# Other query tiles for two units of weight sums, and one catch-up block of the layer norm moved behind the next pair's copies

## The reference

```python
xn = _layernorm(x)
qkv = einsum('bnd,ed->bne', xn, w_qkv)          # q, k, v of width 512
sim = q @ k^T * 512**-0.5, causal; attn = softmax(sim)
s = (attn @ v) @ w_out^T + b_out
h = silu(xn @ wg^T) * (xn @ wu^T)               # hidden 3072, w = int / 127
out = x + s * silu(h @ wd^T)
```

## Time and profile before

| what | value |
|---|---|
| three runs before: median (lowest, highest) | 1453.6 us (1452.38, 1461.93) |
| the profiled execution's own time | 1456.9 us |
| its span (slowest core, first to last instruction) | 1455.3 us |
| outside the span | 1.6 us |
| VectorE, ScalarE, GpSimd busy | 48%, 23%, 14% |
| DMA, mean | 188 GB/s, 273.82 MB |

### The profile page before, as it was taken

How to read it: one execution, slowest core, us unless ns; L and a number is a source line. 1 busy time by engine, 2 the same in 40 slices (tenths; PEclk the granted TensorE clock), 3 DMA queues, 4 the chain that set the end, 5 groups by cost and what they waited for, 6 DMA issues and landing times.

```text
span 1455.3 us, 26205 instructions; the slowest of 8 cores (1435.5 to 1455.3 us)
## 1 busy us (share of the span) xinstructions
PE 1419.7 (98%) x10610; PEld 970.7 (67%) x10610; DVE 691.6 (48%) x989; ACT 334.9 (23%) x435; POOL 196.6 (14%) x248
## 2 busy tenths in 40 slices
PE   8999999999949999999999999999999999999998
PEld 5454444456636677888745888845888845888843
DVE  6652333254413433575713575713576613566613
ACT  5762111222101120232201232201232201222201
POOL 2895000011212211000003000003000003000002
PEclk9999999999979999999999999999999999999999
DMA  6747885269898868755669555569655569654544
GB/s 181 228 167 176 220 210 169 82 147 182 196 147 204 206 182 260 276 154 152 190 215 297 181 146 157 178 219 293 188 151 149 177 225 293 187 157 146 154 136 145
DMA packets 115993, 273.82 MB, mean 188 GB/s; under 512 B 42593, under 2 KB 53089, under 8 KB 112546
## 3 DMA queue, kind: packets, MB, share of 16 engines
q1 hardware_dynamic: 90626, 186.15, 44.1%
q0 software_dynamic: 17280, 76.56, 19.3%
q10 hardware_dynamic: 7968, 9.44, 2.3%
HBM read 218.24 MB, written 64.49 MB: 194 GB/s over the span
## 4 chain that ended last, share of the span: by engine, by line
PE 92%; DMA 3%; DVE 2%; issue 1%; ACT 1%; POOL 0%; DVEq 0%; ACTq 0%; SPq 0%; POOLq 0%
PE ps L237 91%; DMA pT_lo<-p_lo 2%; PE ps L360 1%; DMA wst_scr<-tb 1%; DMA sx<-x 0%; DMA ring<-wst_scr 0%; DVE st L323 0%; DVE st L324 0%; POOL wst_scr L89 0%; DVE xnT_lo L228 0%; DVE tb L228 0%; DVE d_s L228 0%; ACT xnT_hi L223 0%; ACT s_sp L223 0%; DVE negmax L640 0%
## 5 line engine op out<-in xcount | busy, mean ns | idle before, releaser
L237 PE MATMUL ps<-xs,ring 128*128 128x256 f16 x5376 | 587.5, 273 | 0.7 <-DMA ring<-wst_scr 0.7
L237 PEld LDWEIGHTS ps<-xs,ring 128*128 128x128 f16 x5376 | 525.9, 98 | 62.7 <-issue 1.2
L237 PE MATMUL ps<-ring,hA_hi 128*128 128x512 f16 x672 | 254.7, 379 | 0.0
L237 PE MATMUL ps<-ring,hA_lo 128*128 128x512 f16 x672 | 254.7, 379 | 0.0
L237 PEld LDWEIGHTS ps<-ring,hA_lo 128*128 128x128 f16 x672 | 65.8, 98 | 78.9
L237 PEld LDWEIGHTS ps<-ring,hA_hi 128*128 128x128 f16 x672 | 65.8, 98 | 78.8
L237 PE MATMUL ps<-pT_hi,v_hi 128*128 128x128 f16 x544 | 93.3, 221 | 18.9 <-DMA pT_lo<-p_lo 18.9
L237 PE MATMUL ps<-xnT_hi,wqh 128*128 128x512 f16 x256 | 97.0, 379 | 0.0
L237 PE MATMUL ps<-xnT_lo,wqh 128*128 128x512 f16 x256 | 97.0, 379 | 0.0
L237 PE MATMUL ps<-xnT_hi,wql 128*128 128x512 f16 x256 | 97.0, 379 | 0.0
L228 DVE TENSOR_TENSOR hA_lo<-fh,hA_hi 128x1536 f16<-128x1536 f32 (+1 forms) x48 | 95.2, 2017 | 1.8 <-ACT hA_hi L223 1.8
(11 more groups left out here) (122 smaller groups left out, 1587.3 us busy)
## 6 DMA issues: line engine op xcount, KB each, us to landing
ring<-wst_scr SPq DMA_DIRECT2D x252, 512.0 KB, 3.9
pb<-wprep POOLq DMA_DIRECT2D x18, 1024.0 KB, 10.0
xs<-xs_scr POOLq DMA_DIRECT2D x7, 1792.0 KB, 13.7
wst_scr<-tb POOLq DMA_DIRECT2D x44, 256.0 KB, 4.1
wst_scr<-pb POOLq DMA_DIRECT2D x33, 256.0 KB, 3.1
xs_scr<-s_sp SPq DMA_DIRECT2D x16, 512.0 KB, 4.8
sscr<-stl SPq DMA_DIRECT2D x16, 512.0 KB, 3.7
sx<-sscr POOLq DMA_DIRECT2D x32, 256.0 KB, 5.3
```

The lines of the kernel that those rows point to most:

```text
L237: return k.op("te", lambda e: e.matmul(out, lhsT, rhs, start=start, stop=stop, skip_group_check=shared), inc=inc)
```

## The change

Two edits. The set of iterations that make a unit is another, {1, 3, 4, 6, 7, 9, ..., 14} for {2, 4, 6, 7, 8, ..., 14}; both have eleven. And the block ahead of the loop over z is now a function, called in the loop's first half (z = 2, h = 0) behind `evac_ve(2, 0)`; in it `ln_stats(3, h)` of both halves stands ahead of `sums_split(0)`, and `ln_factors(3, h)` behind it.

```diff
-    keep_odd(1)
-    sums(1)
-    sums_split(0)
-    for h in range(2):
-        ln_stats(3, h)
-        ln_factors(3, h)
-    wq_load(0)
-    wq_load(1)
+    def catch_up():
+
+        keep_odd(1)
+        sums(1)
+        for h in range(2):
+            ln_stats(3, h)
+        sums_split(0)
+        for h in range(2):
+            ln_factors(3, h)
+        wq_load(0)
+        wq_load(1)
 
     for z in range(2, NP + 1):
...
                 evac_act(z, h)
                 evac_ve(z, h)
+            if z == 2 and h == 0:
+                catch_up()
             if z + 1 < NP:
                 ln_apply(z + 1, h)
...
-    unit_at = {2, 4, 6, 7, 8, 9, 10, 11, 12, 13, 14}
+    unit_at = {1, 3, 4, 6, 7, 9, 10, 11, 12, 13, 14}
```

## The result

| what | time |
|---|---|
| the changed kernel, median of 11 runs | 1447.95 us |
| the kernel before, in the same comparison, median of 11 | 1457.33 us |
| the same two medians over the runs that the ratio uses, 8 and 9 | 1446.2 and 1455.4 us |
| ratio, with its 95% interval | 0.9927, 0.99 to 0.9954 |
| the changed kernel's profiled execution | 1446.5 us, span 1444.9 |

So the kernel is faster, by 0.7% (0.5 to 1.0) rather than the 1.1% forecast, and the median of the eleven lies 3 us above the range.

A forecast was written before the change was run, and what follows sets the result against it. TensorE's waits on the slowest core were taken to bound the kernel. Core 0, last at 1439.6 - 2.75 - 2.3 = 1434.5, plus 0.9 for remaining waits and 1.6 outside the span, gave 1437.0 us (chance 0.55), range 1432 to 1445.

The forecast's parts named there:

- What bounds the kernel: TensorE, busy 98% of the span, and the slowest core; one wait at tile 9, 18.63 us on core 7, explains the spread.
- Part 1, removal: Without tile 8's unit, tile 9's transposes take 12 to 13 us against 12.3 free; core 7 gets back 20.3 us.
- rival (a): At tile 9, the load alone holds the transposes up, keeping 4 to 6 us; about 1440 us; chance 0.17.
- I take 0 for all three: The units moved to tiles 1, 3 and 4 cost TensorE 0 us, with bounds 0 and 3.
- (d): Unit 8's stores land late at tile 4, delaying tile 6's transposes; slower, up to 1459.6 us; chance 0.05.
- the 0.9: An allowance of 0.9 us in the sum for what the worst of eight cores still waits.
- A rest of 0 to 1 us on most cores: What TensorE would still wait for tile 9's transposes; bounds nothing and 8.7 us.
- rival (b): The wait turns up at another tile, 11 or 5 to 7, costing 6.8 us; about 1440 us; chance 0.13.
- Part 2: Moving the layer norm block leaves waits of 1.4 and 1.0 us for one of 3.18; core 7 gains 2.5 us.
- Rival (c): Only the units help; the layer norm wait returns in full before v_part(10), 2.4 us; 1439.4 us; chance 0.1.
- The sum: Core 7 ends at 1432.5, core 2 at 1432.7, core 0 last at 1434.5; with 0.9 and 1.6 added, 1437.0 us.
- as fast as regular DMAs: The skill's phrase on transposes, read as about a microsecond for 0.3 MB; the prediction held 22.7 and 28.9 us against it.

The follow-up runs named there:

- e17: The kernel before, unaltered, run again in the fourth group: 1455.4 us, ratio to before 1.0013 (0.9985 to 1.0041).
- e13: The kernel before with only the layer norm block moved, units at their old tiles: 1458.0 us, ratio to before 0.9990 (0.9960 to 1.0019).
- e15: The changed kernel, unaltered, run again in the fourth group: 1439.7 us, ratio to before 0.9917 (0.9885 to 0.9949).
- e11: The changed kernel, unaltered, run again in the third group: 1450.7 us, ratio to before 0.9936 (0.9909 to 0.9963).
- e9: The kernel before with unit 12's load issued behind tile 8's seven stores instead of before them: 1481.7 us (three runs).

## Why the prediction was wrong by eleven microseconds

**What bounds the kernel: right.** Waits on the slowest core. e17 shows the same 19 us wait at the same tile, and every kernel without it was faster on the two chips of groups three and four, while the one that kept it (e13) was not. (e17 is also the measure of what a ratio is worth here: the same kernel against itself gives 1.0013.)

**Part 1, removal: right for tile 9, mechanism and size.** The pair took 10.4 to 12.3 us on seven cores (7.1 on core 1, whose load came late), against the 12 to 13 that I took and the 12.3 free; no more than 0.3 us was lost there on any core. Core 7 did get its 20.3 back. That the stores were half of the cause is what the 1728 pairs show; rival (a), the load alone, is out for waits of this length. (Its sum, 1432 + 5 + 1.6, is 1438.6 and not "about 1440".)

**"I take 0 for all three" (the units at tiles 1, 3 and 4): this is the step that failed.** I priced what the moved units do to VectorE and, in (d), unit 8's stores, and left out the load that goes with them. Unit 10's load now stands 7 to 9 us ahead of tile 6's pair, where before had none until 5.3 us behind its first issue. With the old tiles that pair took 6.1 to 6.9 us in all 80 cases, with the new ones 8.3 to 12.9 in 48. Its free time is 9.6, so 0 to 4.9 us are lost by core in e15, 0.4 to 4.1 in the profiled execution, and 6.3 on the slowest core of e11. My bound was 3. With it fails the 0.9 that the sum allows for what the worst of eight cores still waits: in e15, without any wait at tile 8, the worst core was at 1438.7, 4.2 above the 1434.5 that I had for the last one.

**"A rest of 0 to 1 us on most cores": too narrow, and in the profiled execution bad luck.** I counted the load's effect only at the tile where before showed a wait, and let rival (b) look at tiles 11 and 5 to 7. Another load stands near tile 8's pair (unit 12's now, unit 11's before). On core 1 it cost 8.8 us of waiting and 11.2 between outputs; the other 2.4 are the lower clock behind the wait, 0.50 over 394 to 398 us. Taken out with the 2.3 at tile 6 it leaves core 1 at 1431.4. Rival (b) is thus what happened in the profiled execution, at a tile that I hadn't listed; I had priced it at 6.8 us and 1440.

But the change didn't bring that meeting. Twelve executions have such a load at tile 8, 96 pairs, half with the old tiles. Issued 0.5 to 1.5 us behind the first transpose it goes with pairs of 11.4 to 14.4 us (14 pairs), at 1.9 to 2.4 with 7.2 to 8.5 (9), and later with 4.7 to 5.7 in 68 of 71. All of these are within the free time of 14.4. Only two of the 96 caused a wait: core 1 here (23.2 us, load at +2.5) and core 7 of e9 (32.3, old tiles, +0.3). The load came less than 2 us behind in 7 of the 48 pairs with the old tiles and in 10 of the 48 with the new. Why core 1's pair took 23.2 us, when others at +2.5 took 4.7 to 7.0, stays open. What it shares with every other pair over 14 us is that the stores came (at +9.4) before it had landed.

**Part 2: right to a tenth.** Waits of 1.40 and 0.86 for 1.4 and 1.0, at full clock; 59.15 - 38.40 = 20.75 us between the transpose groups for 20.6, on core 0 58.97 - 38.23 = 20.74 for 22.94 before. On the fourth chip the same distance is 20.7 us on all eight cores of e15 and 22.9 to 23.2 on those of e17: 2.2 to 2.5 gained, as predicted. (The mean first output lies 2.6 us ahead, 289.3 for 291.9, but 0.7 of that was there before the moved block is reached.) Rival (c) is out.

**The sum.** Its parts for core 7: predicted 1432.5, measured 1439.0. The first output came at 294.0, 3.4 later than 293.1 - 2.5, with the granted clock at 0.86 over 70 to 90 us; tile 6 cost 1.7; the ring's wait was 1.9 for 0.7. Together 6.3 of the 6.5. Core 0 came out 4.0 under its 1434.5: the 3.9 us that it waited on g_s (2.9) and the ring (1.0) in before didn't recur. I had taken such waits as fixed to a core; here they fall on other cores at each execution (the ring's: cores 0, 2, 5 and 7 in before, 3, 5 and 7 in the changed kernel's profile, 0, 2, 3, 5 and 6 in e15), and the worst of eight collects them.

**The clock, and the 11 us.** Nothing in the prediction allowed for the 0.81. On the fourth chip, which held the full clock from 30 to 290 us, the changed kernel took 1439.7; with the forecast's ratio, 1437.0 / 1453.6 = 0.9886, it would have been 1434.8. So some 5 us are the small waits above. In the main comparison the 11 us from 1437.0 to 1447.95 come apart like this: before stood at 1455.4 there and not at the 1453.6 that I was shown (1.8), the changed kernel 7.4 above what the forecast's ratio makes of that (1446.2 for 1438.8), and the median of all eleven runs another 1.8 above that of the eight. What the 7.4 has over the 5 is of the size of the 2.8 that the lower clock costs a core, but only one execution of that comparison has a profile, so this isn't shown.

**What the Trainium skill has on it.** The rows show a pair with a load of another queue beside it at up to 14 us instead of 5 to 7. The skill's "DMA: Bandwidth & Descriptors", Queues, rings and completion order, with its turns packet by packet, foretold that slowing, and tile 9's 10 to 12 us with the load alone agree. It doesn't foretell the 23.2 us of one pair where others, issued alike to 0.1 us, took 5 to 7. On "as fast as regular DMAs" (the skill's "Advanced Engine Details and Errata", X-Bar Transpose) I was too hard, since the two rows I held against it had a load beside them. With nothing beside it a transpose of tile 8 (9 x 128 x 128 numbers of two bytes, 0.29 MB) landed in 3.4 us. The first store of 256 KB of a unit lands in 2.3 us here, and SP's plain transfers of 512 KB in 3.7 (median). So the trace agrees only roughly, for a transfer that is alone. Of a transpose in company that section gives no figure.

## What to carry to other kernels

When a wait on a DMA is the longest, look at which transfers stand beside it, and hold one kind of them until the awaited one has landed; here it took a load and a row of stores together to make 20 to 30 us out of 5. Moving work to other iterations also moves its transfers, so every iteration in which they come within some 10 us of an awaited one must be priced, those without a wait now included. One profiled execution can show a rare meeting as if it were the rule: look at the same spot on all cores and in several executions before calling it the effect of a change. For a time that is the slowest of eight cores, allow for the small waits and clock losses that land on a different core each time (here 4 to 5 us), even when the big one is gone.

## What the hardware did that I had not expected

- Two transposing transfers of tile 8 took 3.4 us each and 4.8 together when nothing was beside them. With a 1 MB load beside them a pair took up to 13.8 us (683 pairs), with load and stores up to 32.3, and only with both over 14.
- The outcome is not set by the order of issue alone: at tile 8, with the load 2.45 to 2.55 us behind the first transpose, six pairs took 4.7 to 7.0 us and one 23.2.
- Seven stores of 256 KB starting 6.6 us after the first transpose cost it nothing when no load was in flight (5.9 to 7.3 us, e9), since it had landed by then or nearly.
- SP's issue of a second transpose lasted 15.40 us in before, 17.10 in e17 and 18.17 in e9, on core 7 each time, while the first took 22.5 to 23.0 us to land; in a quiet moment it lasts 1.3.
- A granted clock of 0.81 for some 15 us in the first 170 us, with TensorE busy throughout, on some cores of some executions. On the first two of the four chips of the experiments the mean clock of a core over its whole span went down to 0.97 or a little lower, and no gain was to be seen.
